# A GRU scan and an attention layer on one core: gate biases put into PSUM by ScalarE instead of matrix products, and both halves of h in one product for the n gate

## The chip, the core and the metric

The kernel runs on one core of one Trainium2 chip. The metric is the device time of one launch in microseconds (us), taken as the median of three runs. Five engines work side by side: TensorE (PE, matrix products; its weight loads are listed apart as PEld), VectorE (DVE), ScalarE (ACT), GpSimd (POOL), and SyncE (SP), which here issues transfers. They tell each other by semaphores when something is ready. Matrix products write into PSUM, which has 8 banks of 512 fp32 columns.

## What is computed

Two layers, each added to its input. The first is a GRU over 128 time steps, for 16 sequences of width 256:

```
def cell(h, x):
    gi = x @ W_ih + b_ih
    gh = h @ W_hh + b_hh
    r = sigmoid(i_r + h_r)
    z = sigmoid(i_z + h_z)
    n = tanh(i_n + r * h_n)
    h_new = (1.0 - z) * n + z * h
x = x + scan(cell)(x)
x = x + block(x)      # adaLN, 16-head attention, gelu MLP
```

Each step needs the h of the step before. Here i_n and h_n (with their two biases) may not be added before r is known, while for r and z everything adds up in one sum. The second layer is a transformer block with 16 heads of width 128 and an MLP of width 1024, each under a layer norm that is scaled, shifted and gated by a condition vector. It works on whole sequences; the value projections are the part of it that can start before the GRU is done.

## The kernel before, in words

All products are made in fp16 with each fp32 number split into a high half and a low half (`whh_hi`, `whh_lo`, and so on); a product is three products, high x high, low x high and high x low. Sequences and half the width lie side by side in the free dimension, so one step of h is a tile of 128 partitions x 32 columns (2 halves of the width x 16 sequences).

The GRU runs in 16 blocks (`NBL`, index r) of 8 steps (`BS`, index s). The time loop is one code sequence per engine, written out in order; nothing is moved by a scheduler. In block r, TensorE does per step:

- `gru_step`: 36 small products with W_hh and h, N = 16 columns each: for each of the gates r, n, z (two 128-row tiles, two halves of the width) `whh_hi`·h_hi and `whh_lo`·h_hi (`high`, L659), and `whh_hi`·h_lo (`low`, L667). Products of h_hi with r and n come first (16, behind a wait on `hhi_ok`), then h_lo's (behind `hlo_ok`), then all of z.
- then work that does not hang on this step's h: a value projection (`value_item`, L554 to L556, six products of N = 256), a transpose of the block before, a piece of the modulation, and a share of the input products of the next block (`x_products`, L574: 36 products of N = 128, one for each gate tile, half and split, shared out over steps 1 to 7 by the table `share`).
- once per block `x_bias` (L561): three products of a one-hot matrix (`pick`) with the bias rows (`gpair`), N = 256, 256 and 512. They start the accumulation in the three banks of the next block with the biases.

Each gate has its own bank, two of each, for even and odd blocks. The bank of n holds pairs (h part, input part) for each column, so its products write every second column of PSUM. The step's other engines:

- ACT: sigmoid of r (L1018, into `zr[:, :, 1]`), sigmoid of z and of -z (L1020, L1021), tanh (L1023), then, in what time is left, copies for other work: `x_high` (L971), `value_out` (L997), `y_high`, and splits of the weights (`piece_high`, L987).
- DVE: a scan over pairs (L1247) that computes state = zr * state + bank with zr = (0, r): it gives h_n at the first place of a pair and r * h_n + i_n at the second, in `npre`. Then zg * h (L1253), a scan over (zz, nu) that writes the new h in fp16 (L1259, `h_hi`), the same scan in fp32 (L1261, `hs`), and h_lo = hs - h_hi (L1264).

After the last step the attention layer follows, one (sequence group, head) after another, with the MLP at the end.

## Time and profile before

| | us |
|---|---|
| median of 3 runs | 726.83 (726.82 to 728.68) |
| profiled execution, its own time | 728.36 |
| its span, first to last instruction | 726.6 |
| TensorE busy | 704.0 (97%) |
| VectorE busy | 501.7 (69%) |
| ScalarE busy | 458.3 (63%) |
| GpSimd busy | 298.6 (41%) |
| mean granted TensorE clock | 0.993 of full |

The span is what the trace covers; 1.8 us of the profiled execution's time lie around it. "Busy" counts the time between an instruction's start and its modelled end, so for TensorE it says that products were in flight, not that the array was full. In a timeline row the first number is the start in us from the span's start, the second the length, then engine, line of the kernel, operation, what is written <- what is read, shapes (partitions x elements), a count if several were merged, and in brackets how long the engine had been idle before and who released it. The small products of one step last 0.17 us each but start some 25 ns apart: TensorE takes the next before the last is out.

### The profile page before, as it was taken

Reading aid. Unit: us, or ns where it says so; the run is one execution under the profiler, and the core shown is the slowest. Engines: PE = TensorE matmul, PEld = TensorE weight load, DVE = VectorE, ACT = ScalarE, POOL = GpSimd, SP = SyncE. Lnnn points to the kernel's source line nnn. Section 1 sums busy time; section 2 is a strip of 40 time slices with the busy share of each in tenths; the row PEclk is TensorE's granted clock in tenths of the full one; section 3 lists DMA queues with packets and bytes.
Section 4 is the critical chain, followed back from the end, with each engine's and each line's share of the span. In section 5 each row is a group of like instructions: output and inputs, shape, how many; then the busy total and the mean of one; then the engine's idle time right before and its main releaser. Section 6 shows DMA issues by size and latency. Waiting matters only on the chain.

```text
span 726.6 us, 23653 instructions
## 1 busy us (share of the span) xinstructions
PE 704.0 (97%) x9324; PEld 496.7 (68%) x9324; DVE 501.7 (69%) x1440; ACT 458.3 (63%) x1589; POOL 298.6 (41%) x334
## 2 busy tenths in 40 slices
PE   6899999999999999999999999999999999999997
PEld 5688899999888987655555656556565565544455
DVE  5667666666666776776767788677976878634643
ACT  4445556566565555667776777877777777755453
POOL 0222222222222222655556566676667665600040
PEclk9989999999999999999999999999999999999999
DMA  7231433344334323664444434444444444300001
GB/s 238 67 118 46 134 104 106 104 118 120 105 104 122 116 72 92 156 142 110 96 96 109 107 91 96 96 108 95 102 96 100 105 96 102 66 8 30 29 17 43
DMA packets 117989, 70.17 MB, mean 97 GB/s; under 512 B 72267, under 2 KB 110327, under 8 KB 117879
## 3 DMA queue, kind: packets, MB, share of 16 engines
q1 hardware_dynamic: 117303, 67.09, 35.8%
q8 instruction: 74, 1.21, 0.7%
q10 hardware_dynamic: 576, 1.57, 0.6%
q14 instruction: 36, 0.29, 0.1%
HBM read 32.98 MB, written 18.87 MB: 71 GB/s over the span
## 4 chain that ended last, share of the span: by engine, by line
PE 94%; DVE 3%; issue 1%; ACT 1%; DMA 1%; DVEq 0%; SPq 0%
PE bank L554 23%; PE bank L556 22%; PE bank L555 22%; PE bank L659 11%; PE bank L574 6%; PE bank L667 5%; PE bank L561 1%; DVE h_hi L1259 1%; PE bank L626 1%; ACT zg L1020 1%; DMA x<-in_x 1%; PE bank L590 1%; DVE nu L1253 1%; PE bank L583 0%; PE bank L603 0%
## 5 line engine op out<-in xcount | busy, mean ns | idle before, releaser
L1060 ACT ACTIVATE prob<-bank,nmx 128x128 f32<-128x128 f32 x256 | 90.4, 365 | 56.7 <-DVE nmx L1332 56.7
L659 PE MATMUL bank<-h_hi,whh_hi 128*128 128x16 f16 x1536 | 111.3, 173 | 7.1 <-DVE h_hi L1259 6.9
L447 POOL TENSOR_TENSOR w_lo<-stage,w_hi 128x320 f16<-128x320 f32 x64 | 52.1, 814 | 154.3 <-DVE h_lo L1264 151.8
L659 PE MATMUL bank<-h_hi,whh_lo 128*128 128x16 f16 x1536 | 108.7, 172 | 0.8 <-issue 0.8
L659 PEld LDWEIGHTS bank<-h_hi,whh_hi 128*128 128x128 f16 x1536 | 92.4, 97 | 17.7 <-DVE h_hi L1259 16.6
L507 POOL TENSOR_TENSOR p_lo<-prob,p_hi 128x512 f16<-128x512 f32 x64 | 74.0, 1157 | 60.4 <-ACT p_hi L1053 33.0
L554 PE MATMUL bank<-y_hi,w_hi 128*128 128x512 f16 x248 | 94.0, 379 | 0.0
L555 PE MATMUL bank<-y_hi,w_lo 128*128 128x512 f16 x248 | 94.0, 379 | 0.0
L556 PE MATMUL bank<-y_lo,w_hi 128*128 128x512 f16 x248 | 94.0, 379 | 0.0
L659 PEld LDWEIGHTS bank<-h_hi,whh_lo 128*128 128x128 f16 x1536 | 91.1, 97 | 1.4 <-issue 1.1
L667 PE MATMUL bank<-h_lo,whh_hi 128*128 128x16 f16 x1536 | 77.1, 172 | 0.2
L1247 DVE TENSOR_TENSOR_SCAN npre<-zr,bank 128x64 f32<-128x64 f32 x128 | 36.6, 286 | 57.5 <-ACT zr L1018 56.3
L516 POOL TENSOR_TENSOR v_lo<-v_full,v_hi 128x512 f16<-128x512 f32 x64 | 73.9, 1155 | 5.1
L1329 DVE TENSOR_REDUCE mx<-bank 128x4 f32<-128x512 f32 x64 | 44.2, 691 | 38.6 <-PE bank L556 38.6
L554 PE MATMUL bank<-w_hi,y_hi 128*128 128x256 f16 x256 | 69.6, 272 | 0.9 <-DVE v_rows L1238 0.7
L556 PE MATMUL bank<-w_lo,y_hi 128*128 128x256 f16 x256 | 69.9, 273 | 0.0
L555 PE MATMUL bank<-w_hi,y_lo 128*128 128x256 f16 x256 | 69.8, 273 | 0.0
L1018 ACT ACTIVATE zr<-bank 128x32 f32<-128x32 f32 x128 | 25.5, 199 | 68.8 <-PE bank L667 67.9
L1068 ACT ACTIVATE four<-bank,small 128x512 f16<-128x512 f32 x64 | 43.9, 686 | 32.3 <-PE bank L556 30.7
L997 ACT ACTIVATE v_rows<-bank 128x256 f32<-128x256 f32 x118 | 45.2, 383 | 28.4 <-PE bank L556 28.4
L514 POOL CAST v_hi<-v_full 128x512 f16<-128x512 f32 x64 | 39.2, 613 | 46.8 <-DVE nmx L1332 42.4
L667 PEld LDWEIGHTS bank<-h_lo,whh_hi 128*128 128x128 f16 x1536 | 56.4, 96 | 0.4 <-DVE h_lo L1264 0.4
(154 smaller groups left out, 2122.0 us busy)
## 6 DMA issues: line engine op xcount, KB each, us to landing
v_full<-v_spill SPq DMA_DIRECT2D x64, 256.0 KB, 2.9
v_spill<-v_rows SPq DMA_DIRECT2D x28, 512.0 KB, 3.9
stage<-in_weights SPq DMA_DIRECT2D x16, 640.0 KB, 3.9
x<-in_x SPq DMA_DIRECT2D x16, 128.0 KB, 3.9
v_spill<-v_rows SPq DMA_DIRECT2D x16, 128.0 KB, 2.6
out<-xr SPq DMA_DIRECT2D x3, 512.0 KB, 3.1
xr<-in_ada_r SPq DMA_DIRECT2D x1, 1024.0 KB, 7.6
pT_hi<-p_hi SPq DMA_TRANSPOSE x64, 2.4
```

The lines of the kernel that those rows point to most:

```text
L447: gtt(w_lo[:, j * PC:(j + 1) * PC], stage[:, r % 2, i * PC:(i + 1) * PC], w_hi[:, j * PC:(j + 1) * PC], sub).then_inc(piece_lo, 1)
L507: gtt(p_lo[:, d % 2, :], flat_prob[d % 2], p_hi[:, d % 2, :], sub).then_inc(p_l, 1)
L516: gtt(v_lo[:, d % 4, :], v_full[:, d % 2, :], v_hi[:, d % 4, :], sub).then_inc(v_l, 1)
L554: mm(ps, w[0], a[0], start=start, stop=False, skip_group_check=True)
L555: mm(ps, w[1], a[0], start=False, stop=False, skip_group_check=True)
L556: return mm(ps, w[0], a[1], start=False, stop=stop, skip_group_check=True)
L659: nc.tensor.matmul(out(m0 + m), half[:, k, (m0 + m) * P:(m0 + m + 1) * P], h_hi[:, k * B:(k + 1) * B, 1], start=False, stop=False, skip_gr ...
L667: mm = nc.tensor.matmul(out(m0 + m), whh_hi[:, k, (m0 + m) * P:(m0 + m + 1) * P], h_lo[:, k * B:(k + 1) * B], start=False, stop=k == KD - ...
L997: nc.scalar.activation(v_place(i), v_bank(i), copy).then_inc(v_act, 1)
L1060: op = nc.scalar.activation(prob[:, d % 2, j, :], bank[3][:, j * T:(j + 1) * T], ACT.Exp, bias=nmx[:, j:j + 1], scale=SCALE, accum_out=den ...
L1068: nc.scalar.activation(qT_hi[:, d % 2, :], tall_bank(d, 0)[:, :], ident_f, bias=bT[:, BQ + d % H:BQ + d % H + 1]).then_inc(q_h, 1)
L1329: nc.vector.reduce_max(mx[:, :], bank[3][:, :].rearrange("p (j s) -> p j s", j=QUAD), AX.X).then_inc(s_mx, 1)
```

## The change

- The bias products and all that fed them (`grow`, `ghi`, `gpair`, `sel`, `selrz`, `pick`, one transfer) are gone. GpSimd writes two small fp32 tiles, `seed_rz` (b_ih + b_hh for r and z) and `seed_n` (triples b_hh, 0, b_ih). ScalarE copies them into PSUM four times per block (`seed`, 256, 256, 384 and 384 columns), behind the tanh of steps 0, 2, 4 and 6 (steps 0 to 3 in block 0). For block 0 VectorE does it, ahead of its first other work. Six products of zeros (N = 512) run first on TensorE, and no product in the loop starts an accumulation any more: they all add to what stands in the bank.
- r of both block parities shares bank 2, z bank 3. So that TensorE doesn't write a bank while ScalarE reads or writes it, there are new waits: x products of r and z wait on the sigmoid of this step (`r_ok`, `zz_ok`), each gate's first x product waits on its seed (`seeded`), and the step after a seed waits on it before its first product of that bank.
- The n gate keeps triples (whh_hi·h_lo, everything of h_hi, input part), in two banks for each parity (four steps each). The low half of h is written into the first place of `h_hi`'s pairs, and one product with N = 32 (`both`) does whh_hi with h_hi and h_lo together. The scan runs over triples, 96 elements instead of 64, with zr = (0, 1, r).
- Per step TensorE so issues 32 products with h instead of 36. The order changes: ahead of the wait on `hlo_ok` stand r (8), whh_lo of n (4) and whh_hi of z (4), behind it r (4), `both` (4) and z (8).
- The x products of n are made per half block: 24 of N = 64 in place of 12 of N = 128. They write every third column. The table `share` is new.

```diff
-            def x_bias(n):
-                for ps, at, width in ((r_bank, 0, GB), (z_bank, GB, GB), (n_bank, 2 * GB, 2 * GB)):
-                    nc.tensor.matmul(ps[n % 2][:, 0:BS * width], gpair[:, :],
-                                     pick[:, at:at + width].unsqueeze(1).broadcast_to([GK, BS, width]), start=True,
...
+            def x_products(n, order, t1=0):
+                gates = []
+                for m, k, i, half in order:
+                    gate = m // 2
+                    if m % 2 == 0 and (k, i) == (0, 0):
+                        pe.wait_ge(seeded, 4 * n + gate + 1 + half)
+                    if t1 and gate < 2 and gate not in gates:
+                        gates.append(gate)
+                        pe.wait_ge((r_ok, zz_ok)[gate], t1)
                     w, a = ((wih_hi, xb_hi), (wih_lo, xb_hi), (wih_hi, xb_lo))[i]
+                    c = slice(half * HB * B, (half + 1) * HB * B) if gate == 2 else slice(0, P)
...
+            pe.wait_ge(zeros_ok, 1)
+            for i in (2, 3, 0, 1, 6, 7):
+                nc.tensor.matmul(bank[i][:, :], zeros[:, 0:P], zeros[:, :], start=True, stop=True).then_inc(zero_mm, 1)
...
+                def both(m0):
+                    for m in range(2):
+                        for k in range(KD):
+                            mm = nc.tensor.matmul(n_out(m0 + m)[:, :, 0:2], whh_hi[:, k, (m0 + m) * P:(m0 + m + 1) * P],
+                                                  h_hi[:, k * B:(k + 1) * B, :], start=False, stop=k == KD - 1,
+                                                  skip_group_check=True)
...
                 pe.wait_ge(hhi_ok, t1)
+                if s == 1 and r < NBL - 1:
+                    pe.wait_ge(seeded, 4 * (r + 1) + 1)
                 high(0)
-                high(4)
+                high(4, (1,))
+                if s == SEED_AT[r > 0][1] + 1 and r < NBL - 1:
+                    pe.wait_ge(seeded, 4 * (r + 1) + 2)
+                high(2, (0,))
                 pe.wait_ge(hlo_ok, t1)
                 low(0).then_inc(r_mm, 1)
-                low(4).then_inc(hn_mm, 1)
-                high(2)
+                both(4).then_inc(hn_mm, 1)
+                high(2, (1,))
                 low(2).then_inc(z_mm, 1)
...
-            share = (0, 0, 2, 9, 16, 23, 27, 33, 36)
+            share = (0, 0, 3, 9, 15, 21, 27, 36, 48)
...
+            def seed(n, gate):
...
+                nc.scalar.activation(cols, tile.unsqueeze(1).broadcast_to([P, cols.shape[1], tile.shape[1]]), copy
+                                     ).then_inc(seeded, 1)
...
+                    if r < NBL - 1 and s in SEED_AT[r > 0]:
+                        seed(r + 1, SEED_AT[r > 0].index(s))
```

What this does to the instructions, at two places. First TensorE in step 1 of block 4, from the last product of the value item to the first product of step 2 (xb and wih are the x products, y_hi and w_lo the value item, h_hi the next step). Before:

```order
L556 MATMUL bank<-w_lo,y_hi 128x256
L561 MATMUL bank<-pick,gpair 128x256 x2
L561 MATMUL bank<-pick,gpair 128x512
L574 MATMUL bank<-xb_hi,wih_hi 128x8x16 [waits xp_lo]
L574 MATMUL bank<-xb_hi,wih_lo 128x8x16
L659 MATMUL bank<-h_hi,whh_hi 128x16 [waits hhi_ok]
```

and now:

```order
L561 MATMUL bank<-w_lo,y_hi 128x256
L582 MATMUL bank<-xb_hi,wih_hi 128x8x16 [waits r_ok,seeded,xp_lo]
L582 MATMUL bank<-xb_hi,wih_lo 128x8x16
L582 MATMUL bank<-xb_lo,wih_hi 128x8x16
L670 MATMUL bank<-h_hi,whh_hi 128x16 [waits hhi_ok]
```

The three bias products are gone from between, one x product has come forward from step 2, and the x products wait on the sigmoid of r and on the seed. (L561 now names the value item's last product.) Second TensorE in step 7 of block 3, from the modulation product to the first products of the next step. Before:

```order
L603 MATMUL bank<-small,xr 128x16
L574 MATMUL bank<-xb_hi,wih_hi 128x8x16
L574 MATMUL bank<-xb_hi,wih_lo 128x8x16
L574 MATMUL bank<-xb_lo,wih_hi 128x8x16
L659 MATMUL bank<-h_hi,whh_hi 128x16 [waits hhi_ok]
```

and now:

```order
L611 MATMUL bank<-small,xr 128x16
L582 MATMUL bank<-xb_hi,wih_hi 128x4x16 [waits seeded]
L582 MATMUL bank<-xb_hi,wih_lo 128x4x16
L582 MATMUL bank<-xb_lo,wih_hi 128x4x16
L582 MATMUL bank<-xb_hi,wih_hi 128x4x16
L582 MATMUL bank<-xb_hi,wih_lo 128x4x16
L582 MATMUL bank<-xb_lo,wih_hi 128x4x16
L582 MATMUL bank<-xb_hi,wih_hi 128x4x16
L582 MATMUL bank<-xb_hi,wih_lo 128x4x16
L582 MATMUL bank<-xb_lo,wih_hi 128x4x16
L582 MATMUL bank<-xb_hi,wih_hi 128x4x16
L582 MATMUL bank<-xb_hi,wih_lo 128x4x16
```

Step 7 had 3 products of N = 128 and has 12 of N = 64.

## Rows read from the trace of the kernel before

**Rows 1.** The page's chain that ended last: shares by engine, over the span.
```profile
PE 94%; DVE 3%; issue 1%; ACT 1%; DMA 1%; DVEq 0%; SPq 0%
```

**Rows 2.** Timeline of DVE, scan that writes h_hi, steps of block 6.
```profile
112.06 0.29 DVE L1259 TENSOR_TENSOR_SCAN h_hi<-zz,nu 128x64 f16<-128x64 f32 x1
...
114.31 0.29 DVE L1259 TENSOR_TENSOR_SCAN h_hi<-zz,nu 128x64 f16<-128x64 f32 x1
...
116.27 0.29 DVE L1259 TENSOR_TENSOR_SCAN h_hi<-zz,nu 128x64 f16<-128x64 f32 x1
...
118.58 0.29 DVE L1259 TENSOR_TENSOR_SCAN h_hi<-zz,nu 128x64 f16<-128x64 f32 x1
...
120.54 0.29 DVE L1259 TENSOR_TENSOR_SCAN h_hi<-zz,nu 128x64 f16<-128x64 f32 x1
...
122.58 0.29 DVE L1259 TENSOR_TENSOR_SCAN h_hi<-zz,nu 128x64 f16<-128x64 f32 x1 [0.17 <-ACT nu L1023]
...
124.54 0.29 DVE L1259 TENSOR_TENSOR_SCAN h_hi<-zz,nu 128x64 f16<-128x64 f32 x1
...
126.74 0.29 DVE L1259 TENSOR_TENSOR_SCAN h_hi<-zz,nu 128x64 f16<-128x64 f32 x1
...
128.95 0.29 DVE L1259 TENSOR_TENSOR_SCAN h_hi<-zz,nu 128x64 f16<-128x64 f32 x1
```

**Rows 3.** Timeline of step 1 of block 6: PE, DVE and ACT.
```profile
114.66 0.18 PE L659 MATMUL bank<-h_hi,whh_hi 128*128 128x16 f16 x1
...
114.82 0.19 DVE L1264 TENSOR_TENSOR h_lo<-hs,h_hi 128x32 f16<-128x32 f32 x1
...
115.07 0.36 PE L667 MATMUL bank<-h_lo,whh_hi 128*128 128x16 f16 x8
...
115.36 0.20 ACT L1018 ACTIVATE zr<-bank 128x32 f32<-128x32 f32 x1 [0.50 <-PE bank L667]
...
115.59 0.29 DVE L1247 TENSOR_TENSOR_SCAN npre<-zr,bank 128x64 f32<-128x64 f32 x1 [0.24 <-ACT zr L1018]
```

**Rows 4.** Timeline of PE: bias products, then x products of z, then of n.
```profile
116.33 0.61 PE L561 MATMUL bank<-pick,gpair 44*128 44x256 f16 x3
...
122.57 0.22 PE L574 MATMUL bank<-xb_hi,wih_hi 128*128 128x128 f16 x1
122.63 0.22 PE L574 MATMUL bank<-xb_hi,wih_lo 128*128 128x128 f16 x1
...
126.77 0.31 PE L574 MATMUL bank<-xb_hi,wih_lo 128*128 128x128 f16 x1
126.88 0.31 PE L574 MATMUL bank<-xb_lo,wih_hi 128*128 128x128 f16 x1
```

**Rows 5.** Three lines of DVE: duration in ns min/median/max, first and last start.
```profile
L1247 DVE TENSOR_TENSOR_SCAN npre<-zr,bank x128: 285/286/289, 11.8 to 279.4; 128x64 f32<-128x64 f32 x128
L1264 DVE TENSOR_TENSOR h_lo<-hs,h_hi x128: 191/192/193, 13.0 to 280.6; 128x32 f16<-128x32 f32 x128
L1168 DVE TENSOR_TENSOR xb_lo<-x,xb_hi x2: 418/421/424, 5.9 to 13.1; 128x256 f16<-128x256 f32 x2
```

**Rows 6.** Groups of ACT by shape: busy us, mean ns, idle before.
```profile
L971 ACT ACTIVATE xb_hi<-x 128x256 f16<-128x256 f32 x16 | 6.7, 416 | 1.3 <-DMA x<-in_x 1.3
```

**Rows 7.** Timeline of ACT behind the tanh of step 3 of block 6.
```profile
120.98 0.82 ACT L987 ACTIVATE w_hi<-stage 128x320 f16<-128x320 f32 x2
121.70 0.19 ACT L1018 ACTIVATE zr<-bank 128x32 f32<-128x32 f32 x1
```

**Rows 8.** Stretches of 4 us: busy us and instructions per engine, clock, DMA.
```profile
32.00:36.00 4.00, 2.67 (x81) 2.33 (x81) 3.01 (x14) 1.95 (x12) 1.24 (x2) 1.00 0.84 249
40.00:44.00 4.00, 4.00 (x62) 3.63 (x61) 1.98 (x9) 1.22 (x6) 1.58 (x2) 0.52 0.00 0
52.00:56.00 4.00, 3.03 (x95) 2.69 (x94) 3.13 (x14) 2.03 (x11) 0.67 (x1) 1.00 0.51 186
```

**Rows 9.** Timeline of PE: the first x product of the kernel.
```profile
7.00 0.27 PE L574 MATMUL bank<-xb_hi,wih_hi 128*128 128x128 f16 x1 [1.50 <-DVE wih_lo L1164]
```

More of the change, by code:

```diff
@@ L267, in build, with n_bank, n_step @@
         halves = (slice(0, GATES // 2), slice(GATES // 2, GATES))
-        r_bank, z_bank, n_bank = (bank[0], bank[3]), (bank[1], bank[6]), (bank[2], bank[7])
-        r_cols, z_cols = ([ps[:, 0:BS * GB].rearrange("p (t j) -> p t j", t=BS) for ps in pair]
-                          for pair in (r_bank, z_bank))
-        n_cols = [ps[:, :].rearrange("p (t j s) -> p t j s", t=BS, s=2) for ps in n_bank]
+        r_cols, z_cols = ([ps[:, n * BS * GB:(n + 1) * BS * GB].rearrange("p (t j) -> p t j", t=BS) for n in range(2)]
+                          for ps in (bank[2], bank[3]))
+        HB, STEP = BS // 2, 3 * GB
+        def n_bank(n, half):
+            return bank[(6 if n % 2 else 0) + half]
+        def n_step(n, s):
+            return n_bank(n, s // HB)[:, s % HB * STEP:(s % HB + 1) * STEP]
+        h_lo = h_hi[:, :, 0]
         row_ps, back_ps = bank[5][:, 0:D], bank[5][:, D:2 * D].rearrange("p (k c) -> p k c", k=KD)
@@ L423, in _ @@
         def _(pool):
+            nc.gpsimd.memset(zeros[:, :], 0.0).then_inc(zeros_ok, 1)
             nc.gpsimd.memset(ident[:, :], 0.0).then_inc(ident0, 1)
@@ L615, in _ @@
                     pe.wait_ge(wih_l, 2 * k + half + 1)
-                    x_products(0, [(m, k, i) for m in range(half * GM // 2, (half + 1) * GM // 2) for i in range(3)])
+                    x_products(0, [(m, k, i, late) for m in range(half * GM // 2, (half + 1) * GM // 2)
+                                      for late in range(2 if m > 3 else 1) for i in range(3)])
             before = slice(0, NBL - 1)
@@ L652, in gru_step, with high @@
                 t1 = r * BS + (s + 1)
-                def high(m0):
+                def high(m0, halves=(0, 1)):
                     for m in range(2):
                         for k in range(KD):
-                            for half in (whh_hi, whh_lo):
-                                nc.tensor.matmul(out(m0 + m), half[:, k, (m0 + m) * P:(m0 + m + 1) * P],
+                            for i in halves:
+                                nc.tensor.matmul(out(m0 + m), (whh_hi, whh_lo)[i][:, k, (m0 + m) * P:(m0 + m + 1) * P],
                                                  h_hi[:, k * B:(k + 1) * B, 1], start=False, stop=False,
@@ L689, in gru_step @@
                 pe.wait_ge(hhi_ok, t1)
+                if s == 1 and r < NBL - 1:
+                    pe.wait_ge(seeded, 4 * (r + 1) + 1)
                 high(0)
[L691 removed]
+                high(4, (1,))
+                if s == SEED_AT[r > 0][1] + 1 and r < NBL - 1:
+                    pe.wait_ge(seeded, 4 * (r + 1) + 2)
+                high(2, (0,))
                 pe.wait_ge(hlo_ok, t1)
                 low(0).then_inc(r_mm, 1)
[L694 to L695 removed]
+                both(4).then_inc(hn_mm, 1)
+                high(2, (1,))
                 low(2).then_inc(z_mm, 1)
[L698 to L701 removed]
+            products = [(m, k, i, 0) for m in range(4) for k in range(KD) for i in range(3)]
+            products += [(m, k, i, half) for half in range(2) for m in range(4, GM) for k in range(KD) for i in range(3)]
+            share = (0, 0, 3, 9, 15, 21, 27, 36, 48)
+            share_0 = (0, 0, 12, 20, 24, 28, 36, 42, 48)
+            share_1 = (0, 0, 8, 12, 18, 24, 30, 36, 48)
             for r in range(NBL):
@@ L1178, in _ @@
             dve.wait_ge(hhi_ok, 1)
-            tt(h_lo[:, :], cond_row, h_hi[:, :, 1], ALU.subtract).then_inc(hlo_ok, 1)
+            tt(h_lo, cond_row, h_hi[:, :, 1], ALU.subtract).then_inc(hlo_ok, 1)
             for i, c in enumerate(halves):
```

129 lines of the change are left out of this document (64 added, 65 removed).

## Prediction, before the changed kernel ran

> **What bounds the kernel now.** I began with the chain that ended last [rows 1]: TensorE carries 94% of it, over the whole span. For the attention layer behind step 127 nothing changes, so the question is the GRU, and there "PE is on the chain" can mean two things: the step's own products, which no one can start before h is there, or filler behind them that is still running when h is ready. The timeline tells the two apart by the distance from one h_hi scan to the next [rows 2]. In block 6 the distances are 2.25, 1.96, 2.31, 1.96, 2.04, 1.96, 2.20 and 2.21 us, 16.89 in all. 1.96 us is the floor, seen in three of eight steps here: it is the loop through all engines. Read along [rows 3]: the h_hi scan starts at 114.31, the first product 114.66, h_lo's products 115.07, the sigmoid of r 115.36, the scan over pairs 115.59, and through the tanh the next h_hi scan at 116.27. Every other distance is the floor plus something late:
> - 2.31: step 1, whose filler holds the bias products [rows 4].
> - 2.20, 2.21 and 2.25 (into the next block): steps 5, 6 and 7, whose filler holds x products of n. These start 0.11 us apart where those of z start 0.055 apart [rows 4], with the same N = 128: writing every second column of PSUM takes TensorE twice the time. Step 7 has few x products, but the modulation.
> - 2.04: into step 4. Two weight splits keep ScalarE until the sigmoid of r at 121.70 [rows 7], some 0.09 us later than the floor has it.
>
> So two budgets count per step, the loop and TensorE's filler, and the longer one is paid.
>
> **The change part by part.** The loop first. The number of products ahead of the sigmoid of r stays 16 + 4. Tanh and the h scans stay. The scan over npre grows from 64 to 96 elements. The trace has no scan of another length, so the slope is bounded: a plain two-input operation goes from 192 ns at 32 columns to 421 at 256 [rows 5], 1.02 ns per column, and that line gives 225 at 64; the scan needs 286. If the scan had the same start-up (192 - 33 = 159 ns), its slope is (286 - 159)/64 = 2.0 ns per element, and 32 more cost 0.064 us. The lower end is 0.033 (the plain slope), the upper 0.143 (286/64 for each). I take 0.065: with equal start-up it explains the whole row. The floor becomes 2.02 us.
>
> TensorE's side per step: four products less, at the spacing of [rows 3] (16 in 0.41 us, 0.0256 each): -0.10 us. `both` has 32 columns in place of 16; even at the 0.85 ns per column of the n products it takes 0.027, so I count it as 0.026. A filler that is late by E today is then late by E - 0.10 - 0.065 plus what its own content changes. The x products of n with N = 64 and every third column: I take half of the 0.109 of N = 128, 0.055, as if a step of three cost what a step of two does. The ends are 0.027 (no penalty) and 0.109 (no gain from the halved N). With the new table:
> - step 1, late 0.35 today: bias products gone, -0.43 (1024 columns at the 0.055 per 128 of z), one x product more, +0.055. 0.35 - 0.43 + 0.055 - 0.165 is below zero: floor. Gain 0.29.
> - step 5, late 0.24: three of z and three halves of n (0.33) for one and three (0.38). 0.24 - 0.05 - 0.165 = 0.02: floor, gain 0.16.
> - step 6, late 0.25: nine halves (0.49) for six (0.655). Below zero: gain 0.19.
> - step 7, late 0.29: twelve halves (0.655) for three (0.33). 0.29 + 0.33 - 0.165 = 0.45: it loses 0.22 against today's 2.25, and becomes the longest step of the block.
> - into step 4, late 0.08 by ScalarE: the value item it waits for ends 0.10 sooner and the tanh comes 0.065 later, so the splits start up to 0.165 earlier and the delay goes. Gain 0.02 after the longer floor.
> - the other three steps pay 0.065 each, -0.20.
>
> That is 0.29 + 0.16 + 0.19 - 0.22 + 0.02 - 0.20 = 0.24 us per block, eight times (blocks 3 to 10, which have the modulation) = 1.9. Blocks 11 to 14 have none: today's step 7 is at the floor with some 0.1 us to spare, and 0.33 - 0.1 - 0.165 leaves it late by 0.06. Against today 0.29 + 0.16 + 0.19 + 0.02 - 0.26 - 0.06 = 0.14, plus the backlog of some 0.02 per late step that goes with it: say 0.25 each, 1.0. Blocks 1 and 2: about 0.3 gained together, mostly at the low clock of [rows 8]. Block 0 has little filler and waits on transfers: six steps pay 0.065, +0.4. Block 15 has no x products: +0.05.
>
> The seeds on ScalarE: 256 columns cost about 0.42 us [rows 6], 384 about 0.53 at its slope. They stand behind the tanh, in the stretch that ends with the next sigmoid of r, 1.1 us later, and share it with the value copy of 0.38; steps 0, 2, 4 and 6 have no weight split, so it fits. What is new is that step 1 waits on the seed of step 0 before its first product. The seed starts as the tanh ends and takes 0.42; h_hi is ready 0.45 after the same point, so it is covered by some 0.03 to 0.1 us. Without that cover it would cost at most 0.1 per block, 1.5 in all. In block 0 the seed stands behind an x split of 0.42, and nothing covers it: +0.3, once. The new waits of the x products on r_ok and zz_ok stand behind the value item (six products, 0.65 us); where there is none the step is at the floor and has slack for them.
>
> The beginning: the x products first wait on VectorE [rows 9], which now writes four seeds ahead of its splits, some 1.6 us of work that may or may not be done while x is still on its way. Bounds +0.5 and, if the products of zeros raise the clock sooner, -1.0. I take 0.
>
> Sum: -1.9 - 1.0 - 0.3 + 0.4 + 0.05 + 0.3 = -2.5; with the small backlogs in blocks 3 to 10 (0.02 in three steps each, 0.5) -2.9. Against the profiled execution: 728.36 - 2.9 = 725.4. That execution lay 1.5 above the median of the runs shown, 726.83, so the time to expect for the median is 723.9.
>
> The chip's notes speak against both of my durations on VectorE. In the Trainium skill, "Vector Engine (DVE) Microarchitecture Reference", section "Measured stream behaviour on trn2", built-in operations with one or two sources are said to grow by 1.04 ns per column; by that rule the longer scan would cost 0.033 and the sum be 3 us lower, 720.9. The trace disagrees as to the scan's level [rows 5], 286 against 225 for such a line at 64, but no run shows its slope. The same section says that a port that steps over words pays about 0.65 of a cycle per element. h_lo is now written to every second place: 32 elements, an estimate from that page of some 0.02 us a step. In the trace the operation already reads two stepped sources and lies within 4 ns of the line of unstepped ones, so I count nothing.
>
> **The rivals.**
> - A, the scan's slope is the plain one. The floor becomes 1.99, and about 105 steps at the floor gain 0.032 each: 723.9 - 3.4 = 720.5. For it: all other VectorE rows. Against it: the 61 ns that the scan lies above their line.
> - B, the loop gets one more link: h_lo ends at 115.01 and its products start at 115.07 [rows 3], so there is no slack. If the stepped write, or the seed in step 1, adds 0.02 us to each step, it costs 2.4: 726.3, no change.
> - C, the clock. Ahead of a fall TensorE was busy 2.67 of 4 us; at 3.03 of 4 it kept the high one [rows 8]. A step has now 0.10 us less work for it. At the low level (1.2 GHz) 62 products went through in 4 us where 95 did, a loss of 1.4 us. One more such stretch in blocks 1 to 3 gives 725.3.
> - D, slower: a step of three columns in PSUM costs more than a step of two. The place is the x products of n, above all step 7, where all twelve lie on the path. From 0.055 to 0.068 us each the gain of 2.9 is used up; at 0.082 (half as much again as I take) step 5 is late too and the loss is 8 us against the forecast: 731.8. For it: a step of two doubled the time. Against it: if pairs of columns are what is written at once, a step of three can cost no more than a step of two.
>
> **How the numbers follow.** The forecast has 0.52, its own range 722.2 to 725.6. A 0.13, B 0.10, C 0.12, D 0.13. The range for 8 in 10 takes in A and most of B and C and leaves D's far end out: 720.2 to 728.5. 0.3% of the time, about what a measurement of this kernel can tell from no change, is 2.2 us, so "faster" starts at 724.65: 0.7 of the forecast, all of A, a little of C: 0.51. "Slower" is D and a rest of B and C: 0.16. The remainder, 0.33, is no change.
>
> **What the profile after would show.** Distances between h_hi scans of 2.02 us at the floor (1.99 would be A, over 2.04 B); the npre scan at 350 ns; in a block with modulation, one long distance of 2.4 to 2.5 us from step 7 to the next block and no other above 2.06; x products of n 0.055 us apart (D if 0.068 or more); the sigmoid of r in step 4 no longer late. A third stretch at half clock would be C. I am wrong altogether if the first product of step 1 waits on ScalarE in each block, or if a step in the middle of the block is late because a seed pushed the sigmoid of r back.

## The result, and the profile of the changed kernel

| | before | after |
|---|---|---|
| median of 11 runs each, same chip, us | 727.04 (726.47 to 728.68) | 731.04 (727.26 to 732.47) |
| profiled execution / its span, us | 728.36 / 726.6 | 728.64 / 726.8 |
| mean granted TensorE clock, profiled execution | 0.993 | 0.982 |
| the same, all runs (before: its 63 runs beside the experiments) | 0.982 to 0.993 | 0.975 to 0.985 |

The ratio of after to before is 1.0044, 95% interval 1.0029 to 1.0059. That is 3.2 us slower; the two medians lie 4.0 us apart (727.04 to 731.04). The forecast was 2.9 us faster, and the time lies outside both of its ranges. Note that the profiled execution of after is one of its two quickest: 728.64 at clock 0.982, while nine of eleven stand at 0.975 to 0.979 and 729.9 to 732.5, and the quickest, 727.26, at 0.985. That is a first sign of where to look.

The chain's shares by engine, the answer to [rows 1]:

```profile
PE 82%; DVE 7%; ACT 7%; issue 2%; DMA 1%; DVEq 0%; POOL 0%
```

TensorE's filler is no longer last in most steps: the chain runs through VectorE and ScalarE, that is through the loop. The h_hi scans of block 6, against [rows 2]:

```profile
114.63 0.29 DVE L1306 TENSOR_TENSOR_SCAN h_hi<-zz,nu 128x64 f16<-128x64 f32 x1 [0.26 <-ACT nu L1064]
...
117.12 0.29 DVE L1306 TENSOR_TENSOR_SCAN h_hi<-zz,nu 128x64 f16<-128x64 f32 x1 [0.27 <-ACT nu L1064]
...
119.16 0.29 DVE L1306 TENSOR_TENSOR_SCAN h_hi<-zz,nu 128x64 f16<-128x64 f32 x1 [0.26 <-ACT nu L1064]
...
121.20 0.29 DVE L1306 TENSOR_TENSOR_SCAN h_hi<-zz,nu 128x64 f16<-128x64 f32 x1 [0.26 <-ACT nu L1064]
```

One long distance, 2.49, out of step 7, and seven of 2.04 to 2.05: the form that was forecast. The floor itself is 2.04, not 2.02. What the loop is made of, over all steps: the scan over triples, h_lo, then ScalarE's sigmoid of r and tanh.

```profile
L1294 DVE TENSOR_TENSOR_SCAN npre<-zr,bank x128: 352/354/355, 13.2 to 280.7; 128x96 f32<-128x96 f32 x128
L1311 DVE TENSOR_TENSOR h_hi<-hs,h_hi x128: 196/198/201, 14.4 to 281.9; 128x32 f16<-128x32 f32 x128
...
L1058 ACT ACTIVATE zr<-bank 128x32 f32<-128x32 f32 x128 | 27.4, 214 | 64.5 <-PE bank L678 64.4
L1064 ACT ACTIVATE nu<-npre 128x32 f32<-128x32 f32 x128 | 31.7, 247 | 5.6 <-DVE npre L1294 0.3
```

The same two lines of ScalarE in the trace of before, min/median/max in ns:

```profile
L1018 ACT ACTIVATE zr<-bank x128: 189/200/202, 11.4 to 279.1; 128x32 f32<-128x32 f32 x128
L1023 ACT ACTIVATE nu<-npre x128: 232/233/236, 12.2 to 279.7; 128x32 f32<-128x32 f32 x128
```

The scan went from 286 ns [rows 5] to 354, the sigmoid of r from 200 to 214, the tanh from 233 to 247. The last two now write or read every third word in place of every second; beside that only the bank changed that the sigmoid reads.

The beginning, PE and DVE, against [rows 9]:

```profile
8.26 0.26 PE L582 MATMUL bank<-xb_hi,wih_hi 128*128 128x128 f16 x1 [4.21 <-DVE wih_lo L1211]
...
5.54 0.76 DVE L1207 COPY bank<-seed_rz 128x256 f32<-128x256 f32 x2 [4.48 <-POOL seed_n L445]
6.20 1.01 DVE L1207 COPY bank<-seed_n 128x384 f32<-128x384 f32 x2
7.12 0.41 DVE L1215 TENSOR_TENSOR xb_lo<-x,xb_hi 128x256 f16<-128x256 f32 x1
7.46 1.96 DVE L1211 TENSOR_TENSOR wih_lo<-xr,wih_hi 128x384 f16<-128x384 f32 x4
```

VectorE sits idle for 4.48 us, until the biases have landed and GpSimd has made the seeds; only then do the splits of x and W_ih follow, and the first x product starts at 8.26 instead of 7.00. The products of zeros did raise the clock sooner, at 4.6 us instead of 9.7, but it fell again from 8.0 to 11.4, just where the x products run. And the stretches of 4 us (PE busy and count, PEld, DVE, ACT, POOL, clock, DMA share, GB/s), against [rows 8]:

```profile
12.00:16.00 4.00, 2.73 (x83) 2.60 (x81) 2.03 (x8) 1.85 (x10) 0.00 (x0) 1.00 0.76 287
...
28.00:32.00 4.00, 2.54 (x70) 2.07 (x69) 3.09 (x14) 2.05 (x11) 1.51 (x3) 0.99 0.00 0
32.00:36.00 4.00, 3.54 (x76) 2.96 (x75) 2.87 (x14) 2.27 (x11) 1.32 (x3) 0.50 0.68 213
36.00:40.00 4.00, 3.15 (x72) 3.01 (x72) 3.12 (x12) 2.38 (x11) 0.38 (x2) 0.50 0.65 246
...
52.00:56.00 4.00, 3.05 (x79) 2.37 (x76) 2.93 (x11) 2.59 (x11) 0.67 (x1) 0.97 0.52 188
56.00:60.00 4.00, 3.96 (x72) 3.24 (x69) 2.97 (x13) 2.20 (x10) 1.66 (x2) 0.50 0.01 2
...
72.00:76.00 4.00, 3.16 (x82) 2.49 (x79) 2.98 (x12) 2.64 (x12) 0.86 (x1) 1.00 0.02 6
76.00:80.00 4.00, 4.00 (x81) 3.61 (x79) 1.77 (x8) 1.70 (x7) 1.58 (x2) 0.57 0.04 10
```

Three stretches after 12 us run at the lower level, 1.2 GHz, where before had two: some 20 us against 10. Each follows a stretch in which TensorE waited much, busy 2.54 to 3.16 of 4 us. The busy time of a stretch alone does not tell whether a fall follows: 12 to 16 with 2.73 us kept the high level here, and before kept it from 52 to 56 with 3.03 us where after fell behind 3.05. The last two lie in blocks 2 and 3, where before had none (its two lie in blocks 0 and 1). The h_hi scans there, in block 2:

```profile
57.59 0.29 DVE L1306 TENSOR_TENSOR_SCAN h_hi<-zz,nu 128x64 f16<-128x64 f32 x1 [0.18 <-ACT nu L1064]
59.69 0.29 DVE L1306 TENSOR_TENSOR_SCAN h_hi<-zz,nu 128x64 f16<-128x64 f32 x1 [0.19 <-ACT nu L1064]
62.83 0.29 DVE L1306 TENSOR_TENSOR_SCAN h_hi<-zz,nu 128x64 f16<-128x64 f32 x1 [0.18 <-ACT nu L1064]
65.30 0.29 DVE L1306 TENSOR_TENSOR_SCAN h_hi<-zz,nu 128x64 f16<-128x64 f32 x1 [0.26 <-ACT nu L1064]
```

3.14 us for a step in place of 2.04. Summed over a block (us from the end of the h_hi scan that closes the block before to the end of its own last one, so eight distances; for block 0 seven, from its first scan on; profiled executions):

| | first scan's end | block 0 | 1 | 2 | 3 | 5 to 7, each | 8 | 12 to 14, each |
|---|---|---|---|---|---|---|---|---|
| before | 12.81 | 15.32 | 17.45 | 16.30 | 16.35 | 16.88 | 17.01 | 16.59 |
| after | 14.22 | 14.54 | 16.57 | 17.79 | 17.88 | 16.79 | 16.79 | 16.42 |

Over all 128 steps the last h_hi scan ends at 281.73 us instead of 280.34. Behind it follow 445.1 us, in before 446.2, though nothing changed there: over the twelve profiled executions of this document that rest goes from 444.7 to 446.6 us. So a profiled execution can differ from another by 2 us outside the GRU, and what varies there stays open.

### The profile page after: what moved, and what is told of

Read it like the earlier page. It is cut to its first block, busy times and chain, and to the rows that moved or that the text cites. A ratio compares the mean times of both kernels' runs of the same rounds, so it can differ in the third digit from the quotient of the medians.

```text
span 726.8 us, 23037 instructions
## 1 busy us (share of the span) xinstructions
PE 697.1 (96%) x8962; PEld 487.4 (67%) x8962; DVE 502.8 (69%) x1442; ACT 491.3 (68%) x1649; POOL 299.5 (41%) x334
## 4 chain that ended last, share of the span: by engine, by line
PE 82%; DVE 7%; ACT 7%; issue 2%; DMA 1%; DVEq 0%; POOL 0%
PE bank L559 21%; PE bank L561 21%; PE bank L560 21%; PE bank L670 9%; PE bank L582 4%; DVE npre L1294 3%; PE bank L678 3%; DVE h_hi L1306 3%; ACT nu L1064 2%; ACT zr L1058 2%; ACT w_hi L1016 1%; PE bank L687 1%; PE bank L635 1%; ACT v_rows L1026 1%; PE bank L598 1%
## 5 line engine op out<-in xcount | busy, mean ns | idle before, releaser
L561 PE MATMUL bank<-y_lo,w_hi 128*128 128x512 f16 x248 | 94.0, 379 | 0.0
L670 PE MATMUL bank<-h_hi,whh_lo 128*128 128x16 f16 x1536 | 86.4, 172 | 0.0
L670 PE MATMUL bank<-h_hi,whh_hi 128*128 128x16 f16 x1024 | 72.4, 172 | 13.9 <-DVE h_hi L1306 10.3
L1294 DVE TENSOR_TENSOR_SCAN npre<-zr,bank 128x96 f32<-128x96 f32 x128 | 45.3, 354 | 50.0 <-ACT zr L1058 49.9
L670 PEld LDWEIGHTS bank<-h_hi,whh_hi 128*128 128x128 f16 x1024 | 54.8, 97 | 31.3 <-DVE h_hi L1306 30.2
L1058 ACT ACTIVATE zr<-bank 128x32 f32<-128x32 f32 x128 | 27.4, 214 | 64.5 <-PE bank L678 64.4
L561 PE MATMUL bank<-w_lo,y_hi 128*128 128x256 f16 x256 | 70.3, 275 | 0.0
L670 PEld LDWEIGHTS bank<-h_hi,whh_lo 128*128 128x128 f16 x1536 | 68.3, 97 | 0.2
L678 PE MATMUL bank<-h_hi,whh_hi 128*128 128x16 f16 x1024 | 63.9, 171 | 0.0
L1306 DVE TENSOR_TENSOR_SCAN h_hi<-zz,nu 128x64 f16<-128x64 f32 x128 | 37.4, 292 | 32.1 <-ACT nu L1064 32.0
L582 PE MATMUL bank<-xb_hi,wih_hi 128*128 128x128 f16 (+1 forms) x256 | 52.0, 238 | 6.7 <-DVE wih_lo L1211 4.2
```

What stands on the lines that cost most here:

```text
L561: return mm(ps, w[0], a[1], start=False, stop=stop, skip_group_check=True)
L582: nc.tensor.matmul(gate_cols(n, m, half), w[:, k, m * P:(m + 1) * P], a[:, n % 2, k, c], start=False, stop=False, skip_group_check=True)
L670: nc.tensor.matmul(out(m0 + m), (whh_hi, whh_lo)[i][:, k, (m0 + m) * P:(m0 + m + 1) * P], h_hi[:, k * B:(k + 1) * B, 1], start=False, stop ...
L678: mm = nc.tensor.matmul(out(m0 + m), whh_hi[:, k, (m0 + m) * P:(m0 + m + 1) * P], h_lo[:, k * B:(k + 1) * B], start=False, stop=k == KD - ...
L1294: nc.vector.tensor_tensor_scan(npre[:, :, :].rearrange("p j s -> p (j s)"), zr[:, :, :].rearrange("p j s -> p (j s)"), n_step(r, s), 0.0, ...
L1306: nc.vector.tensor_tensor_scan(h_hi[:, :, :].rearrange("p j s -> p (j s)"), *gates).then_inc(hhi_ok, 1)
```

## The experiments

Each was timed in five rounds against the kernel before, on the same chip. Runs of before had medians of 727.91 beside the first four, 727.81 beside the next four and 727.62 beside the last two. Where kernels come from different groups the ratios are what compares; between medians alone up to 1 us means little, since the intervals of the ratios are 1.7 to 2.8 us wide in all.

**Order alone (e1_share).** After, with the x products and one weight split dealt out anew.

```diff
-SEED_AT = (0, 1, 2, 3), (0, 2, 4, 6)
+SEED_AT = (0, 1, 2, 3), (0, 2, 3, 5)
...
-            share = (0, 0, 3, 9, 15, 21, 27, 36, 48)
+            share = (0, 0, 9, 12, 22, 32, 36, 45, 48)
...
-                    pieces = (0, 1, 1, 3, 3, 3, 3, 4) if r > 0
+                    pieces = (0, 1, 1, 1, 3, 3, 3, 4) if r > 0
```

> The changed kernel with another table: x products of steps 1 to 7 are 9, 3, 10, 10, 4, 9, 3 instead of 3, 6, 6, 6, 6, 9, 12, the seeds of n stand in steps 3 and 5, two weight splits move from step 3 to 4. Theory 'step 7 is overfull': the distance of 2.49 us from step 7 into the next block (eight times, 0.45 over the floor; 0.09 over it in five more) goes, every step of blocks 4 to 14 lies at the floor of 2.04, a block is 16.33 us, and the kernel is 3.5 to 4.5 us faster than the changed one: 727. Rival 'the loss is elsewhere (clock, floor, beginning)': the long step comes back in another place, for instance where the seeds of n now meet other copies on ScalarE, and the time stays at 730 to 731.

Measured: 724.31 (721.39 to 726.81), ratio 0.9952 (0.9937 to 0.9968). Blocks 5 to 14 take 16.32 to 16.34 us each, every step at 2.04. So the 2.49 of step 7 was the table's doing, and the same change with another table is faster than before. The gain over after, 6.7 us, is more than I expected (3.5 to 4.5) and more than the steps give (4.0 in blocks 4 to 14). Where the other 2.7 us lie is not shown: the profiled execution is the slowest of its runs, 726.81, and has 27 us at the low level. The mean clocks of the runs, 0.980 to 0.993 for after's 0.975 to 0.985, point at the clock.

**Fill, first form (e2_fill).** After, with products that nothing reads at the end of steps in blocks 0 to 3 (N = 128, into the n bank that is free), so that TensorE waits less. The table holds 100 of them, not 71.

```diff
+                    if (r, s) in FILL:
+                        for _ in range(FILL[r, s]):
+                            nc.tensor.matmul(n_bank(r + 1, 1)[:, 0:P], wih_hi[:, 0, 0:P], wih_lo[:, 1, 0:P], start=False,
+                                             stop=False, skip_group_check=True)
```

> The changed kernel with 71 products more (N = 128, their sums are overwritten by the seed that follows) at the end of steps in blocks 0 to 3, each where TensorE now waits for h. Theory 'the clock falls because TensorE has too little to do in blocks 1 to 3': no stretch at 1.2 GHz between 50 and 80 us, blocks 2 and 3 shrink from 17.8 and 17.9 to about 16.5 us, mean clock from 0.98 to 0.99, time 3 to 5 us under the changed kernel's, 727. Rival 'the falls have another cause': the same low stretches and the same 731, or more where an added product is late.

Measured: 729.0 (725.32 to 731.86), ratio 1.0007 (0.9988 to 1.0026). The profiled execution, 725.32, had no low stretch after 11 us, and blocks 2 and 3 were 16.64 and 16.41. Over the twelve runs, the four with a mean clock of 0.995 or more took 725.3 to 726.6, the eight at 0.990 to 0.993 took 727.7 to 731.9. This fill did not hold the clock each time, but it shows a price: 3.8 us between the medians of the two groups (725.7 and 729.6), with the same instructions. I had expected 3 to 5 us under after; by the ratios it was 2.7.

**Beginning (e3_start).** After, with the 12 bias columns in a transfer of their own ahead of x.

```diff
-            sp.dma_start(small[:, :], cols_in).then_inc(small_in, 16)
+            sp.dma_start(small[:, 0:2 * GM], cols_in[:, 0:2 * GM]).then_inc(bias_in, 16)
             load_x(0)
+            sp.dma_start(small[:, 2 * GM:NB + GB], cols_in[:, 2 * GM:NB + GB]).then_inc(small_in, 16)
...
-            pool.wait_ge(small_in, 16)
+            pool.wait_ge(bias_in, 16)
```

> The changed kernel with the 12 bias columns loaded first by a small transfer, then x, then the rest of the small tile. Theory 'the first step is late because x and the biases land later and the four seeds stand ahead of VectorE's splits': VectorE writes the seeds from 4.4 us instead of 5.5, its first split starts before 6.3 instead of 7.1, the first h_hi scan ends at 13.4 or earlier instead of 14.2, and the kernel is 0.8 to 1.2 us faster, 730. Rival 'the low clock at 8 to 11 us holds the beginning': the splits are earlier but the x products still end near 12.4, gain under 0.3.

Measured: 730.79 (728.1 to 731.68), ratio 1.0035 (1.0022 to 1.0049). The first x product starts at 7.59 and the first h_hi scan ends at 13.33 instead of 14.22, the 0.9 us expected; but the median falls by 0.25 only (0.7 by the ratios), within what the runs can tell, where 0.8 to 1.2 was expected. In the profiled execution the low stretches moved (17.1 to 23.9, 30.8 to 44.4, 58.1 to 61.5, 75.1 to 78.6 us) and took what was gained: block 0 takes 15.84 for 14.54, and the last h_hi scan ends at 281.58 for 281.73. The start itself depends on the clock too. The first x product stands at 7.35 to 7.67 us in the kernels with early biases and at 7.80 to 8.26 in those with after's beginning, but the first scan's end goes from 13.09 to 14.67 and from 13.91 to 14.96, later where the clock rose later (e8_best and e7_share_start have the same beginning, with 13.09 and 14.67, and their clocks rose at 10.0 and 13.4).

**Seeds without triples (e4_seed_only).** The kernel before, with its pairs, its banks and, but for step 0 of block 1, its order of products. The bias products are gone: ScalarE copies 256, 256 and 512 columns per block, behind the tanh. It also has the small first transfer of e3_start, which after has not.

```diff
-            sp.dma_start(grow[:, :], gate_rows).then_inc(grow_in, 16)
+            sp.dma_start(small[:, 0:2 * GM], cols_in[:, 0:2 * GM]).then_inc(bias_in, 16)
             load_x(0)
...
+            pe.wait_ge(zeros_ok, 1)
+            for i in (0, 1, 2, 3, 6, 7):
+                nc.tensor.matmul(bank[i][:, :], zeros[:, 0:P], zeros[:, :], start=True, stop=True).then_inc(zero_mm, 1)
...
-            x_bias(0)
...
-                        if s == (1 if r > 1 else 0):
-                            x_bias(r + 1)
...
+                    if r < NBL - 1 and s in SEED_AT[r > 0]:
+                        nc.scalar.activation(*seed_tiles(r + 1, SEED_AT[r > 0].index(s)), copy).then_inc(seeded, 1)
```

> The kernel before with one part of the change alone: biases copied into PSUM by ScalarE (256, 256 and 512 columns behind the tanh of steps 0, 2 and 4), no bias products; pairs in n, own banks for r and z, 36 products per step. Theory: the floor stays 1.96, step 1 falls from 2.31 to the floor, the other steps stay, a block is 0.36 shorter and the kernel 4 to 5 us faster than before: 722.5, or 724 if less work on TensorE brings one more low stretch. Rival 'the copies on ScalarE hold the loop': the sigmoid of r is late in steps 1, 3 or 5 and the gain is used up, 727.

Measured: 724.22 (722.99 to 725.06), ratio 0.9955 (0.9939 to 0.9972). Blocks 5 to 7 are 16.53, 0.35 below before. Its sigmoid of r takes 199 ns, its tanh 234, its scan 287: the longer loop is the triples' alone. This splits the change: the seeds with their early biases gain 3.7 us against their own runs of before (3.3 by the ratio), and from there to after it is a loss of 6.5 (0.0089 of the time, from 0.9955 to 1.0044). That loss holds after's later biases too. Against e3_start, which has them early, it is 5.8 (0.9955 to 1.0035): that is what came with the triples, with the banks shared, the new waits and the new table.

**Fill, second form (e5_fill2).** After, with 4 to 14 such products in 17 steps of blocks 0 to 3, now ahead of the x products and into banks 4 and 5, those of the value items and of the rows (hence a wait for the last copy out of them).

```diff
...
+                        for _ in range(FILL[t1 - 1]):
+                            nc.tensor.matmul(bank[5 if 5 < t1 - 1 < 8 else 4][:, 0:P], wih_hi[:, 0, 0:P], wih_lo[:, 1, 0:P],
+                                             start=True, stop=True)
```

> The kernel after with products that fill TensorE's waits (N=128, into the third n bank, which holds nothing yet; in the two last steps of a block into the bank after it) placed ahead of the x products of the steps that have no value item, in blocks 0 to 3; nothing reads what they write. The numbers of them are 4 to 14 a step. Theory (the low clock of blocks 2 and 3 comes from TensorE's idle time there, and is 2.9 us of the 4.0 us that after lost to before): blocks 1 to 3 at 16.4 us each in every run, no low stretch after 12 us, granted clock 0.995 or more, time 726.5 to 728. Rival (the clock falls for another reason, or the fill delays the chain as much as it saves): the low stretches of 31.9 to 42.1 and 55.8 to 62.6 us stay, or blocks 1 to 3 get longer, 730 to 732.

Measured: 726.73 (724.46 to 728.66, 11 runs), ratio 0.9983 (0.9972 to 0.9995); all runs at clocks of 0.996 to 1.000. Beside it after had 1.0044, and the two intervals lie apart. The stretches of 4 us that in after stood ahead of the first two falls, and those that were low:

```profile
28.00:32.00 4.00, 3.95 (x100) 3.66 (x99) 2.75 (x13) 2.13 (x10) 1.59 (x2) 1.00 0.00 0
32.00:36.00 4.00, 4.00 (x104) 3.67 (x101) 2.79 (x14) 2.44 (x11) 1.36 (x2) 1.00 0.42 104
...
52.00:56.00 4.00, 3.67 (x93) 3.28 (x92) 3.00 (x13) 2.73 (x13) 0.86 (x2) 1.00 0.82 299
56.00:60.00 4.00, 3.76 (x93) 3.33 (x91) 3.02 (x12) 1.95 (x10) 1.11 (x2) 1.00 0.01 2
```

The clock stays at 2.4 GHz, where in after 32 to 36 and 56 to 60 were at 1.2. Blocks 2 and 3 fall from 17.79 and 17.88 to 16.60 and 16.40, and the median by 4.3 us (4.4 by the ratios), with more work in the kernel and none taken out. The theory holds, and the rival (low stretches that stay) is out. The gain is not in the two profiled executions, 728.66 here (the slowest of its runs) and 728.64: what blocks 2 and 3 give back, 2.7 us, goes in the first scan (14.67 for 14.22), in block 0 (15.22 for 14.54), in block 1 (16.79 for 16.57) and in the rest behind the GRU (446.6 for 445.1). Nor is the clock all that varies: at 0.996 to 1.000 these runs still spread over 4.2 us.

**The same fill on seeds without triples (e6_seed_fill).** e4_seed_only with the edit of e5_fill2.

> The kernel before with ScalarE's seeds alone (pairs for n, own banks for the gates, biases loaded early) and the same fill in blocks 0 to 3. Theory: its low stretches at 31.8 to 42.0 and 55.7 to 59.1 us cost 1.5 to 2.5 us of its 724.2; without them 722 to 722.8. Rival (its clock costs nothing, since the chain that bounds it is not TensorE's): 724.2 as without the fill.

Measured: 723.86 (722.84 to 726.63), ratio 0.9953 (0.9936 to 0.9971), against 0.9955 without the fill. A miss: I expected 1.5 to 2.5 us. The low stretches are gone from 24 us on and block 2 is 16.11 for 16.79, but block 0 is 1.5 us longer and block 3 0.1. So the clock's price is not the same for each kernel. What the rows show is that it depends on where the low stretch falls: in after, the 10 us in block 1 left its steps at 2.03 to 2.16, while 6.8 us in block 2 made one step 3.14 and the next 2.47. What makes block 0 longer is said under e9_before_fill.

**Order and beginning together (e7_share_start), and the fill with them (e8_best).** Their edits are those of e1_share, e3_start and e5_fill2.

> The kernel after with the rebalanced order of the block's value items (as in the run of the share alone, 724.3) and with the 12 bias columns loaded by a small first DMA. Theory (the two are independent: the start is 0.9 us earlier, the rest as with the share): 723.4. Rival (the clock's low stretches move and take the gain, as they did when the start alone was changed): 724.3 or more.

> The kernel after with all three: rebalanced order, small first DMA, fill in blocks 0 to 3. Theory: every step at the floor of 2.041 us from the second on: 13.3 + 127 x 2.041 us for the first 128 scans, then the same tail of 445.1 us and 1.8 us around the span: 719.4; with the fill's own delays up to 721. Rival (the clock falls elsewhere all the same): 723 to 724.

Measured: 723.52 (720.88 to 725.17), ratio 0.9938 (0.9920 to 0.9956), and 722.35 (721.10 to 725.62), ratio 0.9930 (0.9913 to 0.9947). With the early start the median is 0.8 us lower than e1_share's, as the theory had it, and the third part gives 1.2 more. The intervals overlap both times, so neither step is shown by itself; the three parts together against after are (1.0044 to 0.9930). But 722.35 is 1.4 to 3 above what I expected: I had counted each step at the floor from the second on, where block 0 took 16.37 behind the first scan for 14.29 (7 x 2.041), and blocks 2 and 4 0.3 over the 16.33 of eight steps. In block 0 TensorE stood still for 0.66 us (see e9_before_fill), and from 20.3 to 23.7 us it ran at the low level.

**The fill on the kernel before (e9_before_fill).** The edit of e5_fill2, 8 products fewer in steps 0 and 9 and 5 fewer in step 8. It answers a question that e5_fill2 leaves: perhaps before would gain as much.

> The kernel before (no part of the change) with the fill of blocks 0 to 3 alone, 8 products fewer where a step has bias products; nothing reads what they write. In the trace of before, low stretches at 19.9 to 23.4 and 37.0 to 43.8 us: block 1 is 17.45 us where blocks 2 and 3 are 16.3. Theory (the clock costs before less than after, since it has more work in the steps): block 1 falls to 16.5 to 16.9, and the time falls by 0.5 to 1.2 us, to 726.6 to 727.3; after with the same fill (726.73) is then level with it, so that the change without the clock is worth nothing either way. Rival (the fill gives before as much as it gave after, 4.3 us): 723.5, and the change would be a loss at a full clock too.

Measured: 728.28 (726.93 to 729.80), ratio 1.0007 (0.9995 to 1.0018), at clocks of 0.996 to 1.000. No gain, where 0.5 to 1.2 us was expected. Block 1 falls by 0.72 as expected (17.45 to 16.73), blocks 2 and 3 rise by 0.24 together, and block 0 rises by 1.51, in two steps: 3.79 for 2.93 and 2.95 for 2.35. Without them the fill would have given before about 0.5. The rival, 4.3 us for before as well, is out. With the clock held up in both, the change stands at 726.73 against 728.28, but less what each lost in block 0 (0.7 and 1.5) that is 726.0 against 726.8, an estimate from profiled executions: level within 1 us.

What the first of the two steps waits for can be read from the traces. TensorE stands still there, longer than in before:

```profile
19.95 0.21 PE L659 MATMUL bank<-h_hi,whh_lo 128*128 128x16 f16 x1 [0.77 <-issue]
```

```profile
19.91 0.23 PE L577 MATMUL bank<-xb_lo,wih_hi 128*128 128x128 f16 x1 [2.02 <-issue]
```

The first row is before's, the second e9_before_fill's; "issue" means that the engine waited for nothing that the profile shows. Six of the twelve traces have this stop in block 0, of 0.34 to 2.02 us (before and e5_fill2, e6_seed_fill, e8_best, e9_before_fill, e10_seed_share), and in each it comes behind TensorE's 220th to 222nd recorded product. In each TensorE goes on 1.3 to 1.5 us after a packet of 16 KB on the queue that the profile calls "instruction" has ended (here 17.50 to 18.53 us, in before 17.53 to 18.57). The other six reach that product later, at 20.1 us or after, and do not stop. So the likeliest reading is that TensorE has run out of its own instructions, and that the fill costs block 0 time because its products bring TensorE to that point sooner (17.72 us for 19.01). No run tests it. The second step lies in the low stretch of 20.6 to 24.0 us, where the six fill products ahead of the x products take 0.80 us and TensorE works without a break from 21.54 us until the next products of h, at 23.52.

**Seeds without triples, with an order of their own (e10_seed_share).** e6_seed_fill, and:

```diff
-SEED_AT = (0, 1, 2), (0, 2, 4)
+SEED_AT = (0, 1, 2), (0, 2, 3)
...
-            share = (0, 0, 2, 9, 16, 23, 27, 33, 36)
+            share = (0, 0, 7, 12, 19, 26, 28, 32, 36)
...
-                    pieces = (0, 1, 1, 3, 3, 3, 3, 4) if r > 0
+                    pieces = (0, 1, 1, 1, 3, 3, 3, 4) if r > 0
```

> The kernel before with ScalarE's seeds alone, the fill, and a new order of the x products: 7, 5, 7, 7, 2, 4, 4 products of steps 1 to 7 in place of 2, 7, 7, 7, 4, 6, 3, the seed of n one step earlier, and one weight split taken out of step 3. Without the order (723.86) steps 5, 6 and 7 of a block end late by 0.24, 0.25 and 0.29 us and step 4 by 0.08, while step 1 leaves TensorE idle for 0.27. Theory (what is late is TensorE's filler, and moving products into step 1 is worth 0.24 us a block, and the split 0.08): blocks 5 to 7 from 16.53 to 16.2, blocks 12 to 14 below 16.0, the time by 0.3 x 12 = 3.6 us to 720 to 721. Rival (the seeds on ScalarE become late, or the x products wait on them): blocks stay above 16.4 and 723 or more.

Measured: 720.72 (720.23 to 723.20), ratio 0.9915 (0.9897 to 0.9933), the fastest of all. Blocks 5 to 7 are 16.27, blocks 12 to 14 15.91. Its chain, and the scans around the start of block 6:

```profile
PE 95%; DVE 2%; issue 1%; ACT 1%; DMA 0%; POOL 0%; DVEq 0%
```

```profile
109.99 0.29 DVE L1277 TENSOR_TENSOR_SCAN h_hi<-zz,nu 128x64 f16<-128x64 f32 x1
112.35 0.29 DVE L1277 TENSOR_TENSOR_SCAN h_hi<-zz,nu 128x64 f16<-128x64 f32 x1
114.31 0.29 DVE L1277 TENSOR_TENSOR_SCAN h_hi<-zz,nu 128x64 f16<-128x64 f32 x1
116.27 0.29 DVE L1277 TENSOR_TENSOR_SCAN h_hi<-zz,nu 128x64 f16<-128x64 f32 x1
```

2.36 out of step 7 and 1.96 behind it: the old floor, and TensorE's filler is again what is late. With its own order and the fill, the kernel without triples is 1.6 us below the best one with them (722.35); both have their biases first. The intervals of the two overlap (0.9897 to 0.9933 and 0.9913 to 0.9947), so it is not shown that one is faster than the other; what is shown is that the triples are not needed to get there.

## Why the prediction was wrong

**What held.** The two budgets, and the reading of filler by what is late at the h_hi scan. Step 7 of a block with modulation was given 2.4 to 2.5 and took 2.49; no other step of block 6 is above 2.06. The x products of n with N = 64 and a step of three start 0.055 us apart, the value taken, so rival D (0.068 or more) is out:

```profile
129.19 0.25 PE L582 MATMUL bank<-xb_hi,wih_lo 128*128 128x64 f16 x1
129.25 0.25 PE L582 MATMUL bank<-xb_lo,wih_hi 128*128 128x64 f16 x1
...
129.58 0.25 PE L582 MATMUL bank<-xb_lo,wih_hi 128*128 128x64 f16 x1
```

From 129.25 to 129.58 there are six of them.

The scan over triples was given 350 ns and took 354: 68 ns for 32 elements, 2.1 each. That refutes rival A, and it shows that the rule by which I had priced 720.9 does not hold for this scan: in the Trainium skill, "Vector Engine (DVE) Microarchitecture Reference", section "Measured stream behaviour on trn2", built-in one- and two-source operations are said to grow by 1.04 ns per column, half of what this scan does, and the section does not name the scan. The same section gives about 0.65 of a cycle per element for a port that hops between regions at every element, and more for small steps; it measured 4-byte words. My estimate from it for h_lo's 2-byte words, some 0.02 us, did not come: h_lo went from 192 to 198 ns. The seed of step 0 was covered in every block but the first (the first product waits 57 ns, as everywhere), and in block 0 it cost 0.28 (a wait of 332 ns for 57), where 0.3 was given. The seeds took 0.37 and 0.48 us, for 0.42 and 0.53. Blocks 12 to 14 gained 0.17 each and blocks 5 to 7 0.10.

**Step that failed 1: the beginning, "I take 0".** It cost 1.4 us (12.81 to 14.22), beyond the bound of +0.5. The bound weighed VectorE's 1.6 us of seeds against x being on its way. What I missed stands ahead of them: VectorE may not write a seed before the biases are in the tile of constants and GpSimd has formed the tiles, at 5.54, and the x transfer itself, now queued behind the constants, let ScalarE split x at 6.16 for 5.44. e3_start gives back 0.9 of it by a smaller first transfer. These are single executions; the first x product alone comes 1.26 us later (7.00 to 8.26), and it too varies, 6.45 in e9_before_fill and 7.80 in e5_fill2. The other bound, -1.0 for a clock that rises sooner, did not come: it rose at 4.6 us and was low again when the x products ran.

**Step 2: the floor, 2.02 for 2.04.** The scan was right; its neighbours were not in the sum. I had written that the sigmoid and tanh stay. They stay in number, but their operands moved to every third word: +0.014 from the sigmoid's start to the scan's, +0.014 from the tanh's start to the next h_hi scan's end, +0.006 from h to the sigmoid and -0.018 in the gap ahead of the tanh. With the scan's 0.068 that is 0.084 for 0.065. Against the 1.96 of before the floor is 2.04 for 2.02; 0.018 x 127 steps is 2.3 us, at most, since a step whose filler is late anyway does not pay it. It is what B (+0.02 a step) priced, by another door: its two causes were the stepped write of h_lo and the seed in step 1, and neither was it.

**Step 3: the clock, rival C at 0.12.** The mechanism stood in the text, with the rows that show it: a step has 0.10 us less work for TensorE, and ahead of each fall to 1.2 GHz TensorE had waited much. Its size and its chance were wrong. The rows did not settle the size: 3.03 of 4 us had kept the level in before, and after fell behind 3.05 and 3.16. I priced one more stretch in blocks 1 to 3 at 1.4 us. The one of block 0 went, two came in blocks 2 and 3, and there cost 1.2 and 1.5 us over the 16.60 and 16.40 of e5_fill2; the one in block 1 grew from 6.8 to 10.2 us. And nine of eleven executions are at lower clocks than the profiled one. e5_fill2 gives the whole: 4.3 us of median. With the other two terms put right, the forecast would be 723.9 + 1.4 + 2.3 = 727.6, against 726.73 measured with the fill; with 4.3 for the clock it would be 731.9, against 731.04. That these sums come within 1 us is in part luck: 723.9 starts from before with its own low stretches, and the fill costs time in block 0. I also gave the direction no weight: work taken from TensorE and a longer loop both leave it waiting more, so more low stretches were the likelier case, not 1 in 8.

**Terms that went the other way.** Block 0 was given +0.7 and gained 0.8: the stop of 0.77 us that before has there (see e9_before_fill) and its low stretch of 19.9 to 23.4 us are both gone. That hides about half of the beginning's loss, and nothing in the prediction foresaw it. Block 1 gained 0.9, where blocks 1 and 2 together were given 0.3, and block 15 lost 0.2 for 0.05. For blocks 11 to 14 the sum itself is wrong: 0.29 + 0.16 + 0.19 + 0.02 - 0.26 - 0.06 is 0.34 and not 0.14, which puts the forecast 0.8 too high. Less the floor's 0.018 x 8 = 0.14 that is 0.20, near the 0.17 that blocks 12 to 14 gave. In blocks 4 to 10 0.3 was given each, and 0.1 came in five and 0.2 to 0.3 in two (16.88 to 16.79, 17.01 to 16.79); the floor's 0.018 x 8 = 0.14 is most of the difference.

**What stays open.** Block 0 varies by 1 to 2 us between kernels that differ little there (14.5 in after, 15.2 in e5_fill2, 16.4 in e1_share). In e5_fill2 TensorE stops for 0.54 us; e1_share has no stop, but low stretches of 17.0 to 27.2 us, and in neither does the profile name a wait of over 0.04 us on a data transfer there. No run separates the two causes. Nor is it shown what decides when the clock rises first, from 4.1 to 13.6 us over the twelve traces. Nor did I measure the stepped access of ScalarE by itself; that it costs 13 to 15 ns rests on the same two operations in after and in e4_seed_only (214 against 199, 247 against 234), which differ in that and, for the sigmoid, in the bank.

## What to carry to other kernels

Taking work off TensorE can cost time when a loop through other engines sets the pace: look at how busy TensorE is left, because a fall of its clock also slows the products on the path, and count every stretch in which it will now wait more, not one. When a layout changes from pairs to triples, list every operation that reads or writes it, and give each its own line in the sum, those that "stay" too. Split a change with two ideas, and give both halves the same beginning: here the copied biases were worth 3.7 us and the triples cost about 5.8, and the table of shares has to be dealt out anew for each version (6.7 us for after, 3 for the one without triples).

## What the runs showed that I had not expected

- Products that nothing reads made a kernel 4.3 us faster (731.04 to 726.73) and did nothing for its neighbour (727.62 to 728.28), though both show low stretches.
- TensorE stops in block 0 behind its 220th to 222nd product in six traces, for 0.34 to 2.02 us, and fill ahead of that point makes the stop longer (0.77 in before, 2.02 with the fill).
- Within one kernel, runs with the same instructions fall into groups by mean clock: 725.3 to 726.6 at 0.995 or more, 727.7 to 731.9 at 0.990 to 0.993 (e2_fill).
- A step of three words costs TensorE no more than a step of two: N = 128 at two 0.109 us apart, N = 64 at three 0.055, so 0.85 ns per column both times, against 0.43 for dense columns. On ScalarE it costs 13 to 15 ns for 32 columns over a step of two.
- VectorE's scan takes 2.1 ns per element (286 ns at 64, 354 at 96), which leaves 150 ns as its start.
